# Score products on 32 rows of the array instead of zero-padded keys, and maxima jobs that fill two banks

## The reference, cut to what matters

```
layer 1: causal attention, one head of 128, rotary positions, softmax, output projection
layer 2: h = rmsnorm(x) @ w_down                       # 64 values
         q, k, v = rope(h @ wq), rope(h @ wk), h @ wv  # 16 heads of 4 values
         s = q @ k.T / 2, masked where key > query; o = softmax(s) @ v
         x = x + o @ w_up
         then 8 experts, top 2 per token: w2[e]( silu(t @ w1[e]) * (t @ w3[e]) ), weighted
```

## Time and profile before

| | |
|---|---|
| median of three runs | 705.74 us (704.86 to 705.88) |
| profiled execution | span 704.1 us, from the first to the last record |
| PE busy | 623.6 us, 89% |
| DVE busy | 510.4 us, 72% |
| ACT busy | 409.8 us, 58% |
| POOL busy | 344.8 us, 49% |
| a steady round | 61.3 to 62.6 us, five of them |
| expert tiles at the end | 552 to 704 us |

### The profile page before, as it was taken

The page is one execution under the profiler, slowest core; times in us unless marked ns, Lnnn a source line. Parts: engine busy times, 40 slices in busy tenths (PEclk is TensorE's granted clock), DMA queues, the critical chain, the costliest instruction groups (busy, mean ns, idle before and its releaser), DMA issues.

```text
span 704.1 us, 15681 instructions
## 1 busy us (share of the span) xinstructions
PE 623.6 (89%) x5090; PEld 409.6 (58%) x5090; DVE 510.4 (72%) x1712; ACT 409.8 (58%) x794; POOL 344.8 (49%) x390
## 2 busy tenths in 40 slices
PE   8987699999999989999998999898978887999980
PEld 3434356556646655564665556455445577899970
DVE  7364967787896888789688878767777456357994
ACT  3234256566556656655665665456525675688971
POOL 4043265158158455815845581444401457567782
PEclk9999999999999999999999999999989999999995
DMA  5201001000110100010010001001511114236652
GB/s 170 78 0 31 1 1 30 2 1 1 35 32 1 31 31 6 1 39 26 2 31 30 6 1 43 24 2 32 188 29 34 48 57 117 84 94 181 173 162 87
DMA packets 40219, 34.19 MB, mean 49 GB/s; under 512 B 6673, under 2 KB 37329, under 8 KB 40129
## 3 DMA queue, kind: packets, MB, share of 16 engines
q1 hardware_dynamic: 35824, 23.84, 12.7%
q0 software_dynamic: 4320, 9.38, 3.9%
HBM read 17.54 MB, written 12.57 MB: 43 GB/s over the span
## 4 chain that ended last, share of the span: by engine, by line
PE 40%; DVE 22%; POOL 18%; issue 12%; ACT 3%; DMA 2%; SPq 1%; DVEq 0%; POOLq 0%; ACTq 0%
DVE nmax L1411 7%; PE small L866 5%; PE wide L886 4%; PE small L911 4%; PE wide L1101 4%; PE small L898 3%; POOL result_rows L1349 3%; PE small L934 3%; PE small L963 3%; DMA result_rows<-k_rows,dest 2%; PE small L870 2%; POOL k_rows L1324 2%; PE wide L891 2%; DVE a_xn L1403 2%; DVE a_st L1392 2%
## 5 line engine op out<-in xcount | busy, mean ns | idle before, releaser
L1411 DVE TENSOR_REDUCE nmax<-small 128x1 f32<-128x512 f32 (+3 forms) x352 | 216.3, 636 | 49.7 <-PE small L870 46.8
L1198 ACT ACTIVATE pT<-wide 128x1024 f32<-128x1024 f32 x160 | 159.2, 1022 | 58.1 <-PE wide L891 57.1
L866 PE MATMUL small<-kz,qT 128*128 128x256 bf16 (+3 forms) x512 | 125.4, 306 | 13.5 <-DVE nmax L1411 13.0
L1340 POOL DMA_INDIRECT token_rows<-m_row,place_u x64 | 62.8, 981 | 118.4 <-DVE place_u L1625 89.4
L886 PE MATMUL wide<-qT,kz 128*128 128x512 bf16 (+3 forms) x512 | 97.6, 304 | 9.5 <-DVE qT L1562 7.9
L1349 POOL DMA_INDIRECT result_rows<-k_rows,dest x71 | 69.3, 976 | 39.0 <-issue 19.7
L870 PE MATMUL small<-future_sb,idb 128*128 128x128 bf16 (+2 forms) x352 | 87.2, 248 | 0.0
L911 PE MATMUL small<-pT,v_pad 128*5 128x512 f32 (+3 forms) x1024 | 76.5, 438 | 0.8 <-issue 0.7
L866 PEld LDWEIGHTS small<-kz,qT 128*128 128x128 bf16 x512 | 44.1, 98 | 48.3 <-DVE nmax L1411 30.6
L886 PEld LDWEIGHTS wide<-qT,kz 128*128 128x128 bf16 x512 | 43.9, 99 | 43.3 <-issue 11.7
L1752 DVE TENSOR_TENSOR a_work<-a_work,wide 128x256 f32<-128x256 f32 x71 | 29.7, 418 | 39.1 <-ACT a_work L1230 15.2
(11 more groups left out here) (250 smaller groups left out, 1285.7 us busy)
## 6 DMA issues: line engine op xcount, KB each, us to landing
a_qkv_sb<-token_rows SPq DMA_DIRECT2D x71, 72.0 KB, 1.9
kz<-k_all SPq DMA_DIRECT2D x32, 128.0 KB, 2.4
x<-L_attn_x SPq DMA_DIRECT2D x8, 256.0 KB, 3.9
kz<-L_ffn_w SPq DMA_DIRECT2D x2, 1024.0 KB, 7.4
kz<-result_rows SPq DMA_DIRECT2D x16, 128.0 KB, 2.3
out<-x SPq DMA_DIRECT2D x16, 128.0 KB
result_rows<-k_rows,dest POOLq DMA_INDIRECT x71, 2.2
token_rows<-m_row,place_u POOLq DMA_INDIRECT x64
```

Of the source, the lines that this page charges most:

```text
L866: pe.matmul(bank[:, at:at + keys], qT1[:, m.parity, g, tile * P:(tile + 1) * P], kz[:, m.parity, g, r, 0:keys], start=(r == r0), stop=Fals ...
L1198: act.activation(pT[:, g % 2, s, :], wide[:, w % 2, :], ACT.Exp, scale=SCALE_B)\
L1340: pool.indirect_dma_start(token_rows[:, :], bass.IndirectOffsetOnAxis(ap=place_u[:, n, t:t + 1], axis=0), m_row[:, n, t, :], None).then_in ...
L1411: ins = dve.tensor_reduce(nmax[:, tile, g * R + r0:g * R + r0 + heads], bank[:, 0:heads * (tile + 1) * P].rearrange("p (h k) -> p h k", h= ...
```

## The change: what it does

- `kz`, its clearing, the copy by SyncE and the waits for them go. The transposed keys stay in `kT`, one copy for each of two batches. The expert weights and part of the results get buffers of their own where they lay on `kz` before.
- A score product reads only the 32 rows of its head, of queries and of keys. The heads of a group form two pairs, heads 0 and 1 and heads 2 and 3.
- A maxima job covers a pair: it fills two banks, one head in each, for tile 3, for tile 2, or for tiles 1 and 0 together. That is 6 jobs a group, 24 a round. Both banks are taken at once, so there is one such buffer, not two. DVE reduces both banks in one instruction, or two where there are two tiles.
- An exponential job covers a pair: tile 0; tiles 1 and 3; tile 2. That is 6 a group, 24 a round; four of six have 1024 scores, two have 512.
- The masks come first, as products of all 128 rows, then the 32-row products add to them. Two jobs written with `&` are one step: their masks, then their products in turn, so that four products on four different row groups follow one another. `m_x1_1&m_e00` is such a step.
- The steady list has 32 score steps, 16 of them with two jobs; LEAD_ORDER has 28 (20), TRAIL_ORDER 26 (22), DRAIN_ORDER 25 (17), SECOND_ORDER 6 (0). The steady lists are new throughout; in the others the remaining steps stand nearly as they stood. `a_xT` moves to the banks of the other jobs.
- `product_v` waits for the last two exponential jobs and reads `pT` by the new layout.

```
-MAX_JOBS = [(3, r, 1) for r in range(R)] + [(2, r, 1) for r in range(R)] + [(1, 0, 2), (1, 2, 2), (0, 0, R)]
-PT_AT = {0: 0, 1: 512, 3: 896}
-EXPS = R + 1
+MAX_JOBS = [(((3, 0),), 0), (((3, 0),), 1), (((2, 0),), 0), (((2, 0),), 1), (((1, 0), (0, 2 * P)), 0), (((1, 0), (0, 2 * P)), 1)]
+EXP_JOBS = [(((0, 0),), 0), (((0, 0),), 1), (((1, 0), (3, 3 * P)), 0), (((1, 0), (3, 3 * P)), 1), (((2, 0),), 0), (((2, 0),), 1)]
+EXPS = len(EXP_JOBS)
+def keys_up_to(tile):
+    return (tile + 1) * P
+def queries_from(tile):
+    return T - tile * P
+def place_of(tile, r):
+    if tile == 2:
+        return 4, (r // 2) * T + (r % 2) * 2 * P
+    return 2 * (r // 2) + (tile != 0), (r % 2) * T + (3 * P if tile == 3 else 0)
...
+        m_shift0 m_x1_0 f_pv2 m_x1_1&m_e00 f_o1 f_pv3 a_xT f_o2 m_x1_2 a_qkv0 a_qkv1 m_x1_3 a_qkv2 a_qkv3 f_o3
+        m_x1_4&m_e01 f_oT p_hT m_x1_5&m_e02 f_up m_x2_0&m_e03 m_shift1 m_e04 a_qT m_x2_1 p_cT m_x2_2&m_e05 a_kT
+        p_qkv0 m_x2_3 p_qkv1 f_tT m_x2_4 a_s0 f_logits m_x2_5&m_e10 a_s1 m_pv0 m_x3_0&m_e11 a_s2 a_s3
+        m_x3_1&m_e12 m_shift2 a_p0 m_x3_2&m_e13 a_p1 p_k0 m_x3_3&m_e14 m_e15 p_k1 p_q0 m_x3_4 f_rank m_e20 p_q1
+        m_x3_5 m_pv1 p_x0&m_e21 m_shift3 m_e22 a_p2 p_x1&m_e23 a_oT p_x2&m_e24 m_e25 m_o0 p_x3&m_e30 a_r
+        p_x4&m_e31 m_e32 p_x5&m_e33 m_e34 m_e35""",
...
+        m_cut0 p_rnorm m_shift0 m_x1_0 a_stats p_stats f_o1 a_norm m_x1_1 f_o2 a_rope m_x1_2 p_norm p_ms m_x1_3
+        f_o3 m_x1_4 m_x1_5 f_up m_cut1 m_x2_0 m_shift1 m_x2_1 f_ms m_x2_2 a_kT m_x2_3 m_x2_4 a_s0 f_logits
+        f_route0 p_rope f_route1 p_cut a_s1 m_x2_5 f_route2 m_cut2 f_route3 m_x3_0 a_s2 a_s3 m_x3_1 m_shift2
+        f_at m_x3_2 a_p1 p_k0 m_x3_3 p_k1 m_x3_4 f_rank m_x3_5 f_count m_cut3 p_x0 m_shift3 p_x1 p_x2 m_o0 p_x3
+        a_r p_x4 a_rstat p_x5""",
...
-    "SP": """
-        p_rows""",
...
-    return job[1:3] == "_x"
+    return job[1:3] == "_x" and job != "a_xT"
...
-        return self.index(job) % 2 + (0 if is_max(job) else 2)
+        return 0 if is_max(job) else 2 + self.index(job) % 2
     def turns(self, job):
-        return self.index(job) // 2
+        return self.index(job) if is_max(job) else self.index(job) // 2
...
-        k_all = sb("k_all", [P, G, T], BF16)
-        kz = sb("kz", [P, 2, G, R, T], BF16)
+        kT = sb("kT", [P, 2, G, T], BF16)
         qT1 = sb("qT1", [P, 2, G, T], BF16)
...
-                    if step == "p_rows":
-                        if first(p):
-                            sp.wait_ge(fills, N_FILLS)
-                        c = sp.compute_val(ring.count("p_k1"))
-                        sp.wait_ge(half_done, 1)
-                        sp.wait_ge(small_free[ring.bank("p_k1")], c)
-                        for r in range(R):
-                            sp.dma_start(kz[32 * r:32 * r + 32, p.parity, :, r, :],
-                                         k_all[32 * r:32 * r + 32, :, :]).then_inc(kz_in, 16)
...
-            def max_job(m, ring, g, n):
...
-            def exp_job(m, g, s):
...
+            def head_rows(r):
+                return slice(32 * r, 32 * r + 32)
+            def max_masks(m, ring, g, n):
                 job = max_name(g, n)
+                blocks, pair = MAX_JOBS[n]
+                take(ring, job, ["p_k0", "p_k1", "p_q0", "p_q1"] if (g, n) == (0, 0) else ())
+                lo = blocks[0][0] * P
+                for i in range(2):
+                    pe.matmul(small[:, i, lo:lo + len(blocks) * P], idb[:, :], future_sb[:, 0:len(blocks), :],
+                              start=True, stop=False, skip_group_check=True)
+            def exp_masks(m, g, s):
                 w = g * EXPS + s
+                blocks, pair = EXP_JOBS[s]
                 wait(pe, wide_free[w % 2], wide_turns(m, w))
+                for i in range(2):
+                    bank = wide[:, w % 2, i * T:(i + 1) * T]
+                    diagonal = bank.rearrange("p (n k) -> p n k", k=P)[:, 0:NT:3, :] if len(blocks) > 1 else bank[:, 0:P]
+                    pe.matmul(diagonal, idb[:, :], future_T[:, :, :] if len(blocks) > 1 else future_T[:, 0, :],
+                              start=True, stop=False, skip_group_check=True)
+            def max_product(m, g, n, block, i):
+                blocks, pair = MAX_JOBS[n]
+                rows = head_rows(2 * pair + i)
+                tile, at = blocks[block]
+                keys = keys_up_to(tile)
+                return pe.matmul(small[:, i, at:at + keys], qT1[rows, m.parity, g, tile * P:(tile + 1) * P],
+                                 kT[rows, m.parity, g, 0:keys], start=False, stop=True, skip_group_check=True)
+            def exp_product(m, g, s, block, i):
+                w = g * EXPS + s
+                blocks, pair = EXP_JOBS[s]
+                rows = head_rows(2 * pair + i)
+                tile, at = blocks[block]
+                at += i * T
+                return pe.matmul(wide[:, w % 2, at:at + queries_from(tile)], kT[rows, m.parity, g, tile * P:(tile + 1) * P],
+                                 qT2[rows, g % 2, tile * P:T], start=False, stop=True, skip_group_check=True)
+            def scores(ring, p, m, step):
+                names = step.split("&")
+                maxima = [((p if j[0] == "p" else m), 0 if j[0] == "p" else int(j[3]), int(j.split("_x")[1].split("_")[-1]))
+                          for j in names if is_max(j)]
+                exps = [(m, int(j[3]), int(j[4])) for j in names if not is_max(j)]
+                for job in exps:
+                    _, g, s = job
+                    if s == 0:
+                        pe.wait_ge(small_free[ring.bank(f"m_shift{g}")], ring.count(f"m_shift{g}"))
+                    exp_masks(*job)
+                for of, g, n in maxima:
+                    max_masks(of, ring, g, n)
+                for block in range(2):
+                    for job in exps:
+                        blocks = EXP_JOBS[job[2]][0]
+                        for i in range(2 if block < len(blocks) else 0):
+                            last = exp_product(*job, block, i)
+                            if (block, i) == (len(blocks) - 1, 1):
+                                w = job[1] * EXPS + job[2]
+                                last.then_inc(wide_full[w % 2], 1)
+                    for of, g, n in maxima:
+                        blocks = MAX_JOBS[n][0]
+                        for i in range(2 if block < len(blocks) else 0):
+                            last = max_product(of, g, n, block, i)
+                            if (block, i) == (len(blocks) - 1, 1):
+                                full(ring, max_name(g, n), last)
...
-                        act.activation(pT[:, g % 2, s, :], wide[:, w % 2, :], ACT.Exp, scale=SCALE_B)\
-                           .then_inc(wide_free[w % 2], 1)
+                        (tile, _), *more = EXP_JOBS[s][0]
+                        part, at = place_of(tile, 2 * EXP_JOBS[s][1])
+                        in_ = wide[:, w % 2, :].rearrange("p (n q) -> p n q", n=2)[:, :, 0:T if tile < 2 else queries_from(tile)]
+                        n = in_.shape[1] * in_.shape[2]
+                        act.activation(pT[:, g % 2, part, at:at + n].rearrange("p (n q) -> p n q", n=2), in_,
+                                       ACT.Exp, scale=SCALE_B).then_inc(wide_free[w % 2], 1)
...
-            def clear_keys(lo, hi):
-                words = kz[:, :, :, :, :].rearrange("p a g r t -> p (a g r t)").bitcast(F32)
-                pool.memset(words[:, lo:hi], 0.0).then_inc(fills, 1)
...
-                tile, r0, heads = MAX_JOBS[n]
-                bank = await_job(ring, job)
-                ins = dve.tensor_reduce(nmax[:, tile, g * R + r0:g * R + r0 + heads],
-                                        bank[:, 0:heads * (tile + 1) * P].rearrange("p (h k) -> p h k", h=heads),
-                                        AX, ALU.max, negate=True)
+                blocks, pair = MAX_JOBS[n]
+                heads = slice(g * R + 2 * pair, g * R + 2 * pair + 2)
+                await_job(ring, job)
+                for tile, at in blocks:
+                    ins = dve.tensor_reduce(nmax[:, tile, heads], small[:, 0:2, at:at + keys_up_to(tile)],
+                                            AX, ALU.max, negate=True)
...
-                        wait(dve, kz_in, 16 * R * p.n)
                         n = int(step[-1])
                         bank = await_job(ring, step).bitcast(BF16)
                         empty(ring, step, dve.tensor_copy(
-                            k_all[:, 2 * n:2 * n + 2, :].rearrange("p g t -> p (g t)"), bank))
+                            kT[:, p.parity, 2 * n:2 * n + 2, :].rearrange("p g t -> p (g t)"), bank))
```

197 lines of the change are left out of this document (60 added, 137 removed).

## The result

The changed kernel takes 758.0 us (four runs, 754.3 to 761.0) where the kernel before takes 705.3: ratio 1.0745, 95% interval 1.0702 to 1.0788. The forecast was 694 us.

A forecast was written before the change was run, and what follows sets the result against it. PE's instruction stream was taken as the bound, DVE next. Five steady rounds -10, first round -0.7, lead, trail and drain -1.3: -12.0 us in all, giving a median of 694 us, range 670 to 720.

The forecast's parts named there:

- Bound, stream and change of shape: Steady rounds: PE sets the pace; its score stream, shape changes included, takes 23.5 us a round against 24.8.
- an excursion: Each score step's change from 128-row masks to 32-row products and back: 0.25 us, 32 a steady round, 8.0 us.
- the 1.3 of the sum: Steady rounds: PE's score stream, with stagger and shape changes, 1.3 us less a round.
- the 3 to 5 us named as a sign: Sign that the forecast is right: PE busy 3 to 5 us less a steady round in records.
- Rivals 1 and 2: Shape changes hide at 0.08 us each: 669 us, chance 0.18; or are dear at 0.39 us: 722 us, chance 0.17.
- the longer bound of an excursion: Upper bound for changing shape and back in a score step: 0.39 us, both changes waiting for a matmul's tail and a load.
- the 3.73 us: Steady round: product streaming of the 16 steps with two jobs, two of them counted as using the same pair twice.
- The first round, "-0.7": First round: without clearing `kz` beside DVE's mask cast, the rotation starts some 0.7 us earlier.
- The single buffer, "-0.2": Steady rounds: new waits for the one maxima buffer, less waits removed, change PE's waits by -0.2 us a round.
- Rival 3: Steady rounds: 20 of 24 buffer hand-overs stay uncovered, DVE needs 63.4 us, +1.8 a round; 713 us, chance 0.08.
- The other rounds, "-1.3": Lead, trail and drain rounds: 1.3 us less for the three together, with DVE's hand-overs limiting the gain.
- The clock, rival 4: Row groups don't overlap, some 760 us, or quarter-filled products lower the clock, 724 us; chance 0.07.

The follow-up runs named there:

- run 10: Kernel before, with only the products of its 32 single-head maxima jobs a round on 32 rows; ratio 1.0639 to the kernel before.
- run 4: Changed kernel with the lead round alone ordered by the steady list; ratio 1.0612 to the kernel before, 744.0 to 751.5 us.
- run 13: Changed kernel with exponential jobs' mask matmuls issued four times instead of once in rounds without all four stages; ratio 1.0902 to the kernel before.
- Run 5: Changed kernel with its warm-up matmuls on 32 rows in place of 128; 853 us in one execution.
- run 16: Changed kernel with products on all 128 rows of zero-padded keys and maxima reductions reading an eighth of their keys; ratio 1.0211 to the kernel before.
- 14: Changed kernel with each maxima reduction reading an eighth of its keys, products still on 32 rows; ratio 1.0178 to the kernel before.
- run 2: Changed kernel with zero-padded keys, their copies by DMA and products on all 128 rows restored; ratio 1.1285 to the kernel before.
- 15: Kernel before with each maxima reduction reading an eighth of its keys; ratio 0.9607 to the kernel before.
- 17: Kernel before with single-head maxima products on 32 rows and maxima reductions reading an eighth of their keys; ratio 1.022 to the kernel before.

## Why the prediction was wrong

- **Bound, stream and change of shape: right.** PE sets the pace. Products start 0.01 us apart (0.03 taken), an excursion costs 0.20 by the timeline and 0.17 by run 10 (0.25 taken). In the steady round at 0.97 PE is busy 56.4 us for 58.3, and over the five rounds 1.5 us less a round, near the 1.3 of the sum; the 3 to 5 us named as a sign did not come. Rivals 1 and 2 didn't happen. Two slips in the working changed little: the longer bound of an excursion is 0.37 by its own terms (twice 0.17 and 0.03), not 0.39, and three steps, not two, have both jobs on the same pair (p_x1&m_e23 too), which the 3.73 us already count.
- **The first round, "-0.7": right, and lost again.** The cast takes 0.23 us for 3.56, and the rotation starts at 12.56 us for 13.19. The first two rounds together still take 3.0 us more: the waits for the maxima from 45 us on are 7.5 us for 3.1.
- **The single buffer, "-0.2": failed.** This is the step that turned the sum. PE idles 7.0 us in that round (63.34 - 56.38) for 3.0 before; over the five rounds it is 4.5 us more a round, where the sum had 0.2 less. I laid PE's own work against the hand-overs and counted VectorE's queue at one place, 0.6. The two largest waits, 1.35 and 1.25 us, stand at two others, where f_route, a_s1 and m_cut2 are ahead of the reductions, and the softmax is late too (two waits of 0.8 and 0.5 us). The exponential jobs, which the sum put at no wait, stand for 1.1 us a round for their banks. Rival 3 had the mechanism with PE and VectorE in turn, at 713.
- **The other rounds, "-1.3": failed.** Lead and trail lost 21.6 us, and the rest, in which the drain lies, 10.9. In the trail I counted 0.76 us of VectorE standing per hand-over and held 16 of them against its busy time. I left out that PE's work cannot start either: in the run of p_x jobs, at the low clock, the masks of one follow those of the last after 1.9 to 2.3 us. PE waits for the maxima for 11.8 us in the trail (4.3 before) and 10.3 in the lead (0.2 before). The lead list has m_x1_1 behind six steps of the stages a and p on VectorE; in the steady order the lead is 8 us shorter (run 4).
- **The clock, rival 4 at a chance of 0.07: failed too.** I took 1.00 in the steady rounds as a property of the kernel, though the earlier trace rows showed what one wait does. Length times (1 - clock) is the time that a stretch loses if TensorE is the bound all through; summed over the windows it rises from 19 to 74 us, where the kernel lost 51. That is a bound, since run 13 bought clock back and gained nothing. Run 5 shows that the 32 rows have a part in it, run 10 how they prolong a fall; by run 16 against 14 the row groups' shorter stream pays for the clock that goes with it, so there the clock of thin products alone does not make the kernel slower. The Trainium skill, TensorE: Matmul & The Clock Gate, A second HAM failure mode: psum-queue depth-cycling, tells of a kernel whose PE stands briefly between groups as it goes through PSUM banks and so loses clock; these traces agree (0.92 to 0.97 where 1.00 stood). I had cited Part 1 of that page and not this section.

In short: the gain in the stream was real, 7.3 us of busy time over the five steady rounds. The pair jobs took more than that: with full rows, and so without the thin products, the form is still 12.9% (run 2) and, with reductions of an eighth, 6.3% (run 16 over 15) slower than the kernel before. In the changed kernel TensorE is idle for 22.6 us more in the steady rounds, and clock went with it, the more as its products were thin. How the 51 us divide between waits and clock can't be told, as they are not additive, nor how the form's part divides between the one buffer, the coarser jobs and the lists: no run has pair jobs with two buffers.

## What to carry to other kernels

Before a buffer is given up for denser work, lay the consumer engine's whole queue, not only its reads, against each hand-over: the waits come where unrelated work is queued ahead. Where TensorE's clock is 1.00 because it never stands, price each new wait with the clock after it, the more so where its work shrinks to few rows. A stream that is 1.5 us a round shorter is no gain if the waits grow by 4.5.

## What the hardware showed that I had not expected

- 32-row matmuls as warm-up left the clock at 0.66 over the first window (0.93 with 128 rows). With 128-row work near at hand 32-row products ran at 1.00 for whole rounds (runs 10, 17).
- Two and four row groups run side by side with starts 0.01 us apart, and entering and leaving 32-row work costs 0.09 and 0.11 us.
- Some VectorE operations of 0.19 us on 128 x 32 numbers took 0.87 to 0.98 in a stretch where GpSimd was busy for 3.6 or more of every 4 us (374 to 382 us), others between them 0.19; in the trail round, with GpSimd idle, all stood at 0.19. The record shows the two together, not which of GpSimd's work does it.
- The kernel before, 95% PE-busy in its steady rounds, still gained 3.9% when VectorE's reductions shrank to an eighth: 58.8 us a round for 61.5, with 1.5 us less idle and 1.1 less busy time of PE.
